# Folding the first weight groups in a row, products without use in the first pair, and the guard's load between the halves of the last attention output

## What is computed

```python
def _L0_xattn_ref(query, key, value, w_q, w_k, w_v, w_o):
    q = split_heads(query @ w_q); k = split_heads(key @ w_k); v = split_heads(value @ w_v)
    scores = jnp.einsum('bhqd,bhkd->bhqk', q, k) * SCALE
    mask = (k_pos[None, :] <= q_pos[:, None]).astype(scores.dtype)
    scores = scores + (1.0 - mask)[None, None, :, :] * -10000.0
    weights = jax.nn.softmax(scores, axis=-1)
    out = jnp.einsum('bhqk,bhkd->bhqd', weights, v)
    return out.transpose(0, 2, 1, 3).reshape(bsz, q_len, HEADS * HEAD_DIM) @ w_o

def _ffn(xn, rw, W1, W2):
    h = xn * jax.lax.rsqrt(mean(xn * xn) + RMS_EPS) * rw
    return jax.nn.silu(h @ W1) @ W2

x = x + tanh(g_xattn) * _L0_xattn_ref(_layernorm(x), ctx_1024, ctx_1024, ...)
x = x + tanh(g_ffn) * _L0_ffn_ref(_layernorm(x), ...)   # top 2 of 14 routed, 2 shared
```

## Time and profile before

| | us |
|---|---|
| three timed runs, median | 121.04 |
| their lowest and highest | 120.91, 121.61 |
| the profiled execution, device time | 121.5 |
| its span, first to last instruction | 119.7 |
| TensorE busy in the span | 108.7 |
| VectorE, ScalarE, GpSimd busy | 68.8, 59.7, 43.9 |
| mean granted TensorE clock | 0.985 |

### The profile page before, as it was taken

How to read it: one execution, slowest core, us unless ns; L and a number is a source line. 1 busy time by engine, 2 the same in 40 slices (tenths; PEclk the granted TensorE clock), 3 DMA queues, 4 the chain that set the end, 5 groups by cost and what they waited for, 6 DMA issues and landing times.

```text
span 119.7 us, 2370 instructions
## 1 busy us (share of the span) xinstructions
PE 108.7 (91%) x814; PEld 92.0 (77%) x814; DVE 68.8 (58%) x194; ACT 59.7 (50%) x100; POOL 43.9 (37%) x75
## 2 busy tenths in 40 slices
PE   6979999994999999999785989999999999999980
PEld 6867768652478478478484979999999999999980
DVE  0058966669469769869524435999733333333361
ACT  4053778833739579579581569423333323333300
POOL 7703598000000100100100758666666666664000
PEclk9999999999679999999999999999999999999999
DMA  3999999999993000000000000000000000000002
GB/s 93 266 299 344 407 411 417 415 430 435 427 418 132 3 0 0 0 5 0 0 0 0 5 0 5 3 0 3 0 5 0 0 0 0 0 0 0 0 0 77
DMA packets 3169, 13.76 MB, mean 115 GB/s; under 512 B 431, under 2 KB 1007, under 8 KB 2775
## 3 DMA queue, kind: packets, MB, share of 16 engines
q1 hardware_dynamic: 3159, 13.63, 30.2%
HBM read 13.40 MB, written 0.23 MB: 114 GB/s over the span
## 4 chain that ended last, share of the span: by engine, by line
PE 72%; DVE 11%; ACT 7%; DMA 4%; issue 3%; DVEq 0%; ACTq 0%
PE score_ps L723 15%; PE attn_ps L723 7%; PE attn_ps L611 6%; PE ring L716 6%; PE ring L718 5%; PE ring L717 5%; PE ring L585 5%; PE score_ps L542 5%; DMA wkq_space<-in_wkq_dram 4%; PE ring L483 3%; PE ring L511 3%; ACT square_junk L803 3%; PE ring L513 2%; PE ring L512 2%; PE score_ps L536 2%
## 5 line engine op out<-in xcount | busy, mean ns | idle before, releaser
L924 ACT ACTIVATE mixT<-ring 128x896 f32<-128x896 f32 x16 | 14.6, 918 | 26.9 <-PE ring L718 26.9
L723 PE MATMUL score_ps<-w,mixT 128*112 (+1 forms) x160 | 19.1, 273 | 0.2 <-ACT mixT L924 0.2
L723 PEld LDWEIGHTS score_ps<-w,mixT 128*112 128x112 f32 x160 | 18.7, 177 | 0.8 <-issue 0.3
L436 POOL TENSOR_TENSOR h_scale<-h_base,minus_half 112x1 f32<-112x1 f32 x4 | 2.2, 549 | 43.9 <-DVE h_base L1055 43.9
L611 PEld LDWEIGHTS attn_ps<-wkq_space,mixT 128*112 128x112 f32 x128 | 14.5, 179 | 3.5 <-issue 3.5
L1195 DVE SCALAR_TENSOR_TENSOR xn_rows<-score_ps,gates,xn_rows 112x128 f32<-112x128 f32 x36 | 10.2, 345 | 11.5 <-PE score_ps L723 11.3
L611 PE MATMUL attn_ps<-wkq_space,mixT 128*112 128x128 f32 x128 | 15.3, 277 | 0.5 <-ACT mixT L795 0.5
L716 PE MATMUL ring<-hT_hi,w_hi 128*128 128x448 f32 (+2 forms) x36 | 13.9, 385 | 1.5 <-issue 1.4
L401 POOL TENSOR_TENSOR w_full<-w,columns 128x256 f32 (+1 forms) x16 | 9.8, 614 | 12.2 <-PE ring L718 10.5
L718 PE MATMUL ring<-hT_hi,w_lo 128*128 128x448 f32 (+2 forms) x36 | 12.6, 350 | 0.0
L717 PE MATMUL ring<-hT_lo,w_hi 128*128 128x448 f32 (+2 forms) x36 | 12.6, 349 | 0.0
(11 more groups left out here) (133 smaller groups left out, 187.1 us busy)
## 6 DMA issues: line engine op xcount, KB each, us to landing
ctx_all<-in_ctx_dram SPq DMA_DIRECT2D x4, 1500.0 KB, 18.7
w<-in_w_dram SPq DMA_DIRECT2D x2, 1792.0 KB, 27.0
wkq_space<-in_wkq_dram SPq DMA_DIRECT2D x2, 512.0 KB, 5.6
wvo<-in_wvo_dram SPq DMA_DIRECT2D x1, 1024.0 KB, 9.8
w<-in_w_shared_dram SPq DMA_DIRECT2D x2, 256.0 KB, 15.9
ctx_head<-in_ctx_head_dram SPq DMA_DIRECT2D x1, 480.0 KB, 7.9
ctx_headT<-in_ctx_headT_dram SPq DMA_DIRECT2D x1, 224.0 KB, 4.8
x_space<-in_x_rows_dram SPq DMA_DIRECT2D x1, 224.0 KB, 5.1
```

Of the source, the lines that this page charges most:

```text
L723: last = nc.tensor.matmul(dst, hidden[slot][:, c, t * ROWS:(t + 1) * ROWS], w2_chunk(c), start=(c == 0), stop=(c == 1))
L924: nc.scalar.activation(hidden[slot], ring[:, 2 * slot:2 * slot + 2, 0:TOKENS], ACT.Silu).then_inc(S["hidden_ready"], 1)
```

## The change

1. **Fold.** The first `fold_keys` becomes a loop of its own: the four products of group 0, then the four of group 1. The second one and the values keep their turns.
2. **Products in the first pair.** `keep_warm(6)` after each of the two halves of `transpose_probs(0)`.
3. **Last pair, TensorE.** `transpose_guard` moves from inside the odd half of the last `attention_out` to before it. The load of `guard_ok` moves between the even and the odd half; the branch itself comes behind the odd half.
4. **Last pair, ACT.** The squares of batch 7 move from behind `round_rows(0)` to before the evacuations of the C3 jobs.
5. **Last pair, DVE.** The evacuation of C3.0.1 moves from ACT to DVE; `subtract_hi(0)` moves from before the guard's operations to behind its load.

```diff
+DVE_MIX = f"C{PAIRS - 1}.0.1"
-ACT_JOBS = [j for j in RING_JOBS if j in SPLIT_JOBS or j[0] == "C"
+ACT_JOBS = [j for j in RING_JOBS if j in SPLIT_JOBS or (j[0] == "C" and j != DVE_MIX)
...
-            fold_keys(0)
+            pe.wait_ge(wkq_loaded[0], 16)
+            for g in range(2):
+                for i in range(4):
+                    rows = slice(HEAD * g, HEAD * g + HEAD)
+                    c = head_of(g, i) // 2
+                    last = nc.tensor.matmul(ring[:, bank_of(f"A{g}"), i * D:(i + 1) * D],
+                                            wkq[rows, 0, 0, c, :], wkq[rows, 0, 1, c, :],
+                                            start=True, stop=True)
+                last.then_inc(S["ring_filled"], 1)
             keep_warm(FOLD_PRODUCTS, misc_ps[:, 0:P])
...
                     last.then_inc(S["ring_filled"], 1)
+                    if t == 0:
+                        keep_warm(FIRST_PRODUCTS, misc_ps[:, 0:P])
...
-                        if t == PAIRS - 1 and odd == 1 and c == GUARD_AFTER:
-                            transpose_guard()
-                last.then_inc(S["attn_done"], 1)
+                if 1 in parities:
+                    last.then_inc(S["attn_done"], 1)
...
+            pe.wait_ge(S["h_ready"], PAIRS - 1)
+            transpose_rows(0, S["hT_filled"])
+            transpose_guard()
+            attention_out(PAIRS - 1, [0])
             pe.wait_ge(S["guard_ready"], 1)
             ok = pe.value_load(guard_ok[0:1, 0:1], min_val=0, max_val=1)
+            attention_out(PAIRS - 1, [1])
...
                 evacuate_own([f"P{t}.{half}" for half in range(2)])
+                if t == PAIRS - 1:
+                    context_squares([7])
                 evacuate_own([f"C{t}.{bb}.{odd}" for bb in range(2) for odd in range(2)])
...
             round_rows(0, S["hT_filled"], S["hT_hi_ready"])
-            context_squares([7])
...
-                    subtract_hi(0, S["hT_hi_ready"], S["hT_ready"])
+                    evacuate_own([DVE_MIX])
                     dve.wait_ge(S["squares_done"], GROUPS + B)
...
                     ok = dve.value_load(guard_ok[0:1, 0:1], min_val=0, max_val=1)
+                    subtract_hi(0, S["hT_hi_ready"], S["hT_ready"])
```

More of the change, by code:

```diff
@@ L83 @@
 LAST_PRODUCTS = 6
-GUARD_AFTER = 3
+FIRST_PRODUCTS = 6
 FOLD_PRODUCTS = 10
@@ L486, in fold, with fold_last_keys @@
                             last.then_inc(S["ring_filled"], 1)
[L488 to L491, removed]
+            def fold_last_keys():
+                pe.wait_ge(wkq_loaded[1], 16)
+                fold(1, "A", lambda rows, c: wkq[rows, 1, 0, c - 4, :],
+                     lambda rows, c: wkq[rows, 1, 1, c - 4, :])
             def fold_values(n):
@@ L517, in _ @@
                 project_keys(s)
-            fold_keys(1)
+            fold_last_keys()
             for s in range(4, 8):
@@ L596, in transpose_guard, with attention_out @@
                 last.then_inc(S["guard_rows_ready"], 1)
-            def attention_out(t):
+            def attention_out(t, parities=range(2)):
                 if t == 0:
@@ L605, in attention_out @@
                     pe.wait_ge(S["x1_ready"], t)
-                for odd in range(2):
+                for odd in parities:
                     for bb in range(2):
@@ L644, in _ @@
                     scores(t + 1, 1)
[L645 to L648, removed]
+                if t < PAIRS - 1:
+                    attention_out(t)
+            pe.wait_ge(S["h_ready"], PAIRS - 1)
+            transpose_rows(0, S["hT_filled"])
+            transpose_guard()
+            attention_out(PAIRS - 1, [0])
             pe.wait_ge(S["guard_ready"], 1)
             ok = pe.value_load(guard_ok[0:1, 0:1], min_val=0, max_val=1)
+            attention_out(PAIRS - 1, [1])
             with pe.If(ok < 1):
```

## The result

The changed kernel takes 117.74 us (median of 4 runs, 117.72 to 117.94); the kernel before, 121.19 in the same comparison (120.91 to 121.61). The ratio is 0.9716, 95% interval 0.9684 to 0.9749: 3.45 us less. 117.8 was forecast. Those 39 executions fall into three groups by their mean granted clock: 8 at 0.996 or more took 119.4 to 120.3 us, 20 at 0.981 to 0.986 took 121.0 to 121.6, and 11 at 0.972 took 121.6 to 123.6. Differences under 0.3 us are not called shown.

The account below looks back on a forecast made before the run. TensorE's chain (72%) was taken as the bound, with losses at the start, the first pair's clock fall and the last pair's guard. +0.05 - 1.4 - 1.85 = -3.2 from the 121.04 median gives 117.8 us; range 117.2 to 119.5.

Parts of the forecast that it names:

- The fold, +0.05: First fold in a row: group 0 comes no sooner, the longer fold is nearly covered; +0.05 us.
- three signs: Fold: 16 passes in 2.4 or more, ACT evacuates group 0 no earlier, first projection at 8.65 to 8.75.
- The bound of +0.5 for a late clock: Fold: if the clock rises 1 us later, half of group 1's passes run slowly, +0.5 beyond the cover.
- The products, -1.4: First pair: twelve products, hidden in waits, keep TensorE busy; -1.4 us if the clock holds.
- The comparison of busy time: First pair: with products TensorE busy 3.10 of 4 us, like the last pair's 3.12, where the clock stays 1.00.
- Rival (a): First pair: the clock falls all the same; 119.2 us, chance 0.25.
- The last pair, -1.85: Last pair: early flag, load and branch hidden; expert products start at about 63.9, not 65.74; -1.85 us.
- Between the halves 0.1 to 0.2: Last pair: 0.1 to 0.2 us remain between the output's even and odd halves after the load.
- Rival (b): Last pair: the load between the halves empties the array, gap of about 0.9; 118.7 us, chance 0.08.
- what is late next: Last pair: residual at 64.05, normalised rows at 66.15, TensorE wants them at 66.3; gain survives with cover 0.15.
- The forecast -3.2: Whole kernel: fold, products and last pair sum to -3.2 us, giving 117.8 from the median 121.04; chance 0.55.
- Rival (d): Start: the clock comes up late, behind the fold and ten products, possibly the first projections; 122.7 us, chance 0.05.

Follow-up runs that it names:

- Experiment 1: The changed kernel with the first fold's products of group 0 and 1 again in turn; 117.77 us.
- experiment 10: The changed kernel with batch 0's square moved ahead of pair 0's second exponential and TensorE's flag load behind the odd half; 117.50 us.
- experiments 11 and 12: The changed kernel with 12 warm products at the start instead of 38: fold in a row 119.82 us, fold in turns 118.67 us.
- experiment 2: The changed kernel without the 12 products in the first pair; 119.15 us.
- experiment 7: The kernel before with only the 12 products of the first pair added; 119.77 us, beside 121.61 for the kernel before.
- Experiment 4: The changed kernel with TensorE's load of the flag moved from between the halves to behind the odd half; 117.59 us.
- experiment 5: The changed kernel with batch 7's square back behind the rounding on ACT, guard transposes still ahead of the output products; 122.86 us.
- experiment 6: The changed kernel with the evacuation of C3.0.1 back on ACT; 117.91 us.

## Why the prediction came out

**The fold, +0.05: right as a cost, and right for its reason.** Experiment 1 gives 0.03 in the medians. But none of its three signs appeared. The 16 passes took 1.68 and not 2.4 or more, ACT began with group 0 at 6.71 and not at 7.28 or later, and the first projection stood at 8.08 and not at 8.65 to 8.75. All three were worked out for a clock that comes up in the middle of the fold, and here it was up before the fold, as the 3.56 of the warm products shows (4.24 before). Where it came up about as late as before (at 6.9 by the length of the passes, in the profile of experiment 10, whose fold began 0.32 earlier), the 16 passes did take 2.51, and the first projection stood 3.39 behind the fold's start, against 3.18 in the kernel before. A single stream was also priced a little too high: 16 passes at 0.119 make 1.9, and the second group's passes begin inside the first's (at 6.07 of 5.55 to 7.23), because the halves of the array overlap there too. The bound of +0.5 for a late clock is what experiments 11 and 12 found as 0.55. That the profile of the changed kernel shows its first projection 0.57 sooner is no merit of the order: its fold ran at the full clock, the old one's mostly at the low one.

**The start, -0.27 in the trace: not in the sum.** The prediction had no term for a transfer in the start. It read the start as the path of TensorE, ACT and DVE, and that was right for the old profile. Half a microsecond of earlier start, with a landing half a microsecond later than in the old profile, was enough to meet the context of batch 0. Both are luck of the execution and not work of the change, so the 0.27 is no merit of it.

**The products, -1.4: right.** 9.06 against 10.41 is -1.35; experiment 2 gives 1.41 the other way. The 1.84 of experiment 7 holds more than this one fall. They were hidden, as said, at 0.50 each. The reason given was weaker than the result. The comparison of busy time promised 3.10 of 4 us, the trace of the changed kernel has 2.78 in 27 to 31, where nearly all of the first six products lies outside, and also 2.78 in 26.6 to 30.6, where it lies inside. Experiment 4 has a fall behind 3.07 of 3.40, the changed kernel none behind 3.06 in the same place. TensorE's busy time in the profile does not say whether the clock will fall. That the products hold it in the first pair is shown; why they do is not, and there the prediction had luck with its reason. Rival (a), a fall in the first pair all the same, was seen in none of the 12 profiles with the products: in each it is 9.06 or 9.07 from pair 0 to pair 1.

**The last pair, -1.85: right, step by step.** The stretch from the mixing to the last transposes shrank by 1.92 (10.58 to 8.66). Moved by the 1.62 that the last pair came sooner, the changed trace has: the output's start at 60.17 (60.1 said), the flag at 60.95 (61.2), the expert products at 63.73 (63.9), the residual at 64.01 (64.05), normalised rows at 66.11 (66.15), the transposes at 66.25 (66.3). Between the halves 0.1 to 0.2 had been set aside; it was under 0.1 (3.80 against 3.72 in experiment 4). Rival (b) falls with that: the load does not empty the array. The step called "what is late next" holds as well. The normalised rows end at 64.49, the transposes start at 64.63, and the stretch before them is 0.09 longer than it was. Of the moves, experiment 5 shows that the early square carries the gain and that moving the guard's transposes without it would have been slower than before; experiment 4 that the load's place carries none; the trace of experiment 6 that the evacuation on DVE carries about 0.2, which the medians do not secure. The early square with the guard's transposes left in the odd half was not run, nor the subtraction's move by itself.

**The sum.** -0.27, -1.35 and -1.92 make the 3.5 of the span. The forecast -3.2 was 0.3 short of the profile's, and 0.25 short of the medians' -3.45; what is missing has the size of the start's 0.27. That 117.8 met 117.74 so closely is in part the base: it went from the median of three runs, 121.04, where four gave 121.19.

**Rival (d), a slower start by a late clock,** is seen in small: the clock came up at 10.0 in experiment 7, and its first projection stood 3.45 behind the fold's start (9.23 - 5.78), 0.9 more than the 2.54 of the same order at the full clock. That fold has its turns, so the row is not needed for it.

## What to carry to other kernels

A load and a branch on a flag cost nothing if the flag is early and enough products are already queued on TensorE; so look for the operation that makes the flag late, here one square on ACT, and put it into a wait, instead of looking for a place for the load. Moving the consumer forward without its producer turns the same edit into the worst kernel of the study, because TensorE works its list in order, waits, and its clock falls in that wait (experiment 5). And a start that becomes faster should be followed on every engine to the next transfer: a square whose data used to be there became, in some executions, the thing that all waited for.

## What was not expected of the hardware

- The granted clock fell in a second place, among the first experts, in two profiles (70.2 to 73.7 and 67.6 to 71.0), behind stretches in which TensorE was busy 3.06 and 3.07 of 3.40 us. It cost 1.6 us there. In the changed kernel, with 3.06 of 3.40 in the same stretch, it did not fall.
- Passes of products on the two halves of the array overlap even where one half's products all stand ahead of the other's: 16 passes in 1.68 us at the full clock, 1.16 in turns, where a single stream of full height took 3.80 for 32.
- The context of batch 0 landed between 18.2 and 20.3 us after the start in the profiles of kernels that issue the same transfers in the same order.
